# First layer of a two-layer cross-attention kernel: the exponential's scores made ahead of the maxima's scores in every step

## The chip, the cores and the metric

The kernel runs on one core of one Trainium2 chip. The metric is the device time of one execution in microseconds (us). Three runs of the kernel before gave 1755.6, 1747.01 and 1757.85 us, a median of 1755.6 us. The profiled execution that is read below took 1751.12 us, 1749.3 us of them inside the profile's span.

## The reference, cut to what matters

Eight batches of x (256 x 512) and of a context of the same shape go through two layers. Only the first one is touched. It attends along the last axis (512 positions) with 16 heads of 16 channels, and needs from the same weights both the mean and the standard deviation of the values:

```
q = Wq x + bq;  k = Wk ctx + bk;  v = Wv ctx + bv        # 16 heads, d = 16, 512 positions
attn = softmax(where(mask, (q / sqrt(d)) . k, -inf))      # 512 x 512 for each head
mean = attn . v;   ex2 = attn . (v * v)
std  = sqrt(relu(ex2 - mean * mean))
out  = (instance_norm(x) * std + mean) * mask
```

The second layer (self-attention, cross-attention and an MLP on 256 rows of 512 channels) follows and is left as it is.

## The kernel before, in words

**Groups and steps.** The first layer works on groups of four heads: 8 batches x 4 groups = 32 groups (`GROUPS`). A group has 8 steps: two pairs of heads, four blocks of 128 positions each. The program for TensorE is a written-out loop over windows `w` and steps `s` (the loop around lines 541 to 575), with `N = 8 * w + s`. Four sorts of TensorE work stand in it.

- `scores(N)` (line 510): two matmuls, one for each head of a pair, of 64 rows each on the upper and the lower half of the array, queries along the partitions. They fill two of four PSUM banks in turn. VectorE takes the maximum over the keys of each query from them (`maxima`, line 607). `scores(N)` waits until the maxima of step `N - 2` have freed its banks.
- `turned(M)` (line 519), with `M = N - 13`: the same products with the keys along the partitions, and with the negated maximum added through two extra rows of the query tile. Two matmuls of 64 rows, always into the same two banks. ScalarE turns them into the weights (`exponentials`, line 772). `turned(M)` waits until exponential `M - 1` has read the banks. Where `M` is a multiple of four it also waits for the maxima of the group to have come into the query tile by DMA (`s_top`).
- `weighted(M - 1)` (line 533): four matmul records of 128 rows that multiply the values and their squares by the weights of step `M - 1`. It waits for exponential `M - 1`, and at the start of a pair of heads until ScalarE has copied the pair before out of its bank (`v_out`, line 808).
- Items (`items_at`): in some steps one more product comes behind `weighted`. In windows with even `w` the projection of queries (`q`) stands in step 3 and that of keys (`k`) in step 6 (line 487); of values (`v`, line 496) there is one in step 6 of odd windows. In step 1 of each window from 1 on the maxima of the window before are turned by the identity (`turn`, line 501).

**ScalarE's order** (from line 771) is fixed too. In each step: for steps 4 and 7 of even windows first `high_of` (line 793), which takes the projection just made out of PSUM; then the exponential of that step; then what else belongs there, such as `take_values` (line 808), `take_turn` (line 801, which reads the turned maxima), the masks (line 780), or the square roots with two loads of a function table (line 832).

**The way of the maxima.** After group `w - 1` has its eight maxima, VectorE spreads them into `wide`, TensorE turns them in step 1 of window `w`, ScalarE copies the result to `top`, and SyncE's queue moves it by four small DMAs (`tops_in`, line 376) into the query tile. `turned` needs it in step 5 of the same window. On SyncE's queue these DMAs stand behind `rows_out` of the window before (line 342), and every fourth window that stands behind `shares_out`, which waits for a reciprocal on VectorE (line 664); this reciprocal comes behind the maxima of step 5 on that engine.

Before the first `turned` there are only `scores`, items and a few matmuls that fill time (line 540). Behind the last `scores` (`N = 255`) thirteen more steps of `turned` and `weighted` follow, together with the first items of the second layer.

Of the kernel before, what the change touches and what calls it, by code (L numbers as in the profile page):

```python
# [34 lines left out]
DMA = 16  # L35
# [49 lines left out]
def layer0(nc, d, g):  # L85

    GROUPS = NB * NG
# [13 lines left out]
    def items_at(w, s):  # L101

        if s in (3, 6) and w % 2 == 0 and w // 2 + 1 < PAIRS:
            return [("q" if s == 3 else "k", w // 2 + 1, (0, 1))]
        if s == turn_step(w) and 0 <= w - 1 < GROUPS:
            return [("turn", w - 1, (0, 1))]
        if s == 6 and w % 4 == 3 and w + 1 < GROUPS:
            return [("v", (w + 1) // 2, (0, 1))]
        if s == 6 and w % 4 == 1 and w < GROUPS:
            return [("v", w // 4 * 2 + 1, (0, 1))]  # L110
        if s == 4 and w == 0:
            return [("v", 0, (0, 1))]
        return []
# [5 lines left out]
    with ExitStack() as ctx:  # L119
# [3 lines left out]
        def sem(name):  # L123
            return g["whole"].enter_context(nc.semaphore("l0_" + name))
# [59 lines left out]
        s_top = [sem(f"top{p}") for p in range(2)]  # L184
# [6 lines left out]
        s_exp = sem("exp")  # L191
# [51 lines left out]
        def landed(eng, n):  # L243

            for name in "qk":
                eng.wait_ge(s_ring[name][n % RING], loads_of(n) * DMA)
# [22 lines left out]
        def rows_of(i):  # L269

            return slice(ROWS * i, ROWS * (i + 1))
# [183 lines left out]
    def tensor(eng, lead):  # L455
# [49 lines left out]
        def scores(N):  # L505

            n, j, p = N // 8, N % 4, N % 8 // 4
            for i in range(2):
                r = rows_of(i)
                mm = eng.matmul(ps[:, SC + 2 * (N % 2) + i, :], q_rows[r, n % RING, p, P * j:P * (j + 1)],  # L510
                                k_rows[r, n % RING, p, :], start=True, stop=True)
            mm.then_inc(s_score, 1)

        def turned(M):

            n, c, p = M // 8, M % 4, M % 8 // 4
            for i in range(2):
                r = rows_of(i)
                mm = eng.matmul(ps[:, ST + i, :], k_rows[r, n % RING, p, P * c:P * (c + 1)],  # L519
                                q_rows[r, n % RING, p, :], start=True, stop=True)  # L520
            mm.then_inc(s_st, 1)

        def weighted(M):

            n, c, p = M // 8, M % 4, M % 8 // 4
            b, G = n // NG, n % NG
            if c == 0:
                eng.wait_ge(s_sq, 2 * b + G // 2 + 1)
                if 2 * n + p:
                    eng.wait_ge(s_vout, 2 * n + p)  # L530
            eng.wait_ge(s_exp, M + 1)
            for k in range(2):
                mm = eng.matmul(ps[2 * QD * k:2 * QD * (k + 1), VB, :], v[:, c, HG * G + 2 * p + k, :],  # L533
                                prob[:, M % PROBS, k, :], start=(c == 0), stop=(c == DC - 1))
            mm.then_inc(s_pv, 1)

        def busy(count, bank, rows):

            for _ in range(count):
                eng.matmul(ps[:, bank, :], rows[:, 0:P], rows, start=True, stop=True)  # L540
# [6 lines left out]
        for w in range(GROUPS + 2):  # L547
            for s in range(8):
                N = 8 * w + s
                M = N - LAG  # L550
                if w < GROUPS:
                    if w == 0 and s in (0, 4):
                        eng.wait_ge(s_first_in[s // 4], 2 * DMA)
                    if w and s == 0:
                        landed(eng, w)
                    if N >= 2:
                        eng.wait_ge(s_max, N - 1)
                    scores(N)
                if N < 12:
                    busy((0, 0, 3, 2, 0, 8, 0, 7, 0, 0, 1, 1)[N], VB, k_rows[:, 0, 0, :])  # L560
                if 0 <= M < 8 * GROUPS:
                    if M % 4 == 0:
                        eng.wait_ge(s_top[M % 8 // 4], 2 * DMA * (M // 8 + 1))
                    if M:
                        eng.wait_ge(s_exp, M)
                    turned(M)
                if 0 <= M - 1 < 8 * GROUPS:
                    weighted(M - 1)
                lead(w, s, False)
                for x in items_at(w, s):  # L570
                    item(*x)
                lead(w, s, True)
# [311 lines left out]
    def gpsimd(eng):  # L884
# [56 lines left out]
        finish_x(LAST - 1, 1)  # L941

    return {"sync": sync, "tensor": tensor, "vector": vector, "scalar": scalar, "gpsimd": gpsimd}


# [1361 lines left out]
```

## Time and profile before

| | |
|---|---|
| median of three runs | 1755.6 us (1747.01 to 1757.85) |
| profiled execution | 1751.12 us, its span 1749.3 us |
| first layer's steps with `scores` and `turned` together | from 60 to about 608 us of the span |
| TensorE busy in the whole span | 1641.2 us, 94% |
| VectorE, ScalarE, GpSimd busy | 71%, 61%, 30% |

Times in the profile's rows are us from the span's start. A matmul's busy time is its own duration from issue to a modelled end, and neighbours overlap; what an operation costs the engine is the distance from its start to the next one's. A row of the time line merges the neighbours of one kind, so that "x2" is a pair of matmuls that run together. Weight loads are listed as an engine of their own (PEld).

### The profile page before, as it was taken

How to read it: one execution, taken by the hardware profiler on the slowest of the kernel's cores; microseconds unless marked ns; L12 is line 12 of the kernel's file. 1: busy time of each engine (PE TensorE's matmuls, PEld its weight loads, DVE VectorE, ACT ScalarE, POOL GpSimd, SP SyncE). 2: the span in 40 equal slices, each digit the busy share in tenths (PEclk: the TensorE clock that was granted, in tenths of full speed). 3: DMA queues.
4: the chain of work that ended last, by engine and by line, in shares of the span. 5: the costliest groups of instructions: out<-in, count | busy, mean ns of one | idle time of the engine just before them, and what ended most of it. 6: DMA issues, size and time to landing. Idle time of an engine off the chain costs nothing.

```text
span 1749.3 us, 30873 instructions
## 1 busy us (share of the span) xinstructions
PE 1641.2 (94%) x10589; PEld 1130.0 (65%) x10589; DVE 1242.7 (71%) x2758; ACT 1063.7 (61%) x2351; POOL 516.1 (30%) x795
## 2 busy tenths in 40 slices
PE   5999999999998988999999899999999899999999
PEld 3434334333343346788878678888888688888888
DVE  2676877778787838988999889999999762323222
ACT  1466766757666657778877878788887642111111
POOL 0135455654546523233223233333333220000000
PEclk7899999999999998999999999999999899999999
DMA  5555354553544413222233534333333330000000
GB/s 150 165 156 183 114 152 134 172 163 115 153 126 132 150 47 105 67 74 74 70 93 76 131 98 109 92 91 92 91 92 84 93 109 1 25 0 25 0 25 13
DMA packets 112556, 167.97 MB, mean 96 GB/s; under 512 B 27401, under 2 KB 43145, under 8 KB 112273
## 3 DMA queue, kind: packets, MB, share of 16 engines
q1 hardware_dynamic: 88720, 132.55, 26.1%
q0 software_dynamic: 20992, 29.12, 6.7%
q10 hardware_dynamic: 2688, 4.33, 0.9%
q8 instruction: 86, 1.41, 0.3%
q14 instruction: 70, 0.57, 0.1%
HBM read 72.06 MB, written 34.60 MB: 61 GB/s over the span
## 4 chain that ended last, share of the span: by engine, by line
PE 56%; DVE 21%; ACT 7%; issue 6%; DMA 5%; SPq 4%; POOL 0%; ACTq 0%; DVEq 0%; POOLq 0%
PE ps L533 11%; PE ps L1929 9%; PE ps L1903 7%; DVE at_t L1381 4%; DVE at_t L1386 4%; PE ps L510 4%; PE ps L1252 4%; PE ps L1262 4%; PE ps L519 3%; SPq L342 3%; PE ps L1201 2%; DMA ring<-top 2%; PE ps L1908 2%; PE ps L496 2%; ACT at_prob L1589 2%
## 5 line engine op out<-in xcount | busy, mean ns | idle before, releaser
L607 DVE TENSOR_REDUCE nmax<-ps 128x2 f32<-128x1024 f32 x256 | 310.0, 1221 | 144.1 <-PE ps L510 142.7
L772 ACT ACTIVATE prob<-ps 128x1024 f32<-128x1024 f32 x256 | 261.8, 1023 | 147.3 <-PE ps L519 142.8
L1589 ACT ACTIVATE at_prob<-at_t,at_nmax 128x256 f32<-128x256 f32 x512 | 256.6, 506 | 85.6 <-DVE at_nmax L1386 74.8
L533 PE MATMUL ps<-prob,v 128*64 128x512 f32 x1024 | 280.0, 625 | 2.0
L1386 DVE CUSTOM_DVE_ANT_0 at_t<-at_t,at_off 128x256 f32<-128x256 f32 x512 | 233.5, 492 | 8.8
L1747 POOL TENSOR_TENSOR at_low<-at_low,at_high 128x512 fp32r<-128x512 f32 x64 | 86.7, 1355 | 463.9 <-DVE at_high L1415 463.9
L2088 DVE CAST mlp_h_hi<-mlp_h 128x512 fp32r<-128x512 f32 x64 | 28.4, 444 | 213.0 <-ACT mlp_h L2000 179.9
L2000 ACT ACTIVATE mlp_h<-ps,b 128x512 f32<-128x512 f32 x48 | 33.1, 690 | 218.3 <-PE ps L1903 218.3
L510 PEld LDWEIGHTS ps<-ring 64*128 64x128 f32 x512 | 48.5, 187 | 168.1 <-issue 134.5
L1201 PE MATMUL ps<-ident,at_prob 128*128 128x128 f32 x1024 | 156.9, 276 | 0.0
L1381 DVE SCALAR_TENSOR_TENSOR at_t<-ps,mask_self 128x512 f32<-128x512 f32 x192 | 131.2, 684 | 19.5 <-PE ps L1190 19.0
L1190 PE MATMUL ps<-at_k_stack,at_q_stack 96*128 96x256 f32 x512 | 117.5, 312 | 29.1 <-ACT at_prob L1589 26.1
L510 PE MATMUL ps<-ring 64*128 64x512 f32 x512 | 130.2, 506 | 11.5 <-DMA ring<-rows 8.1
L519 PE MATMUL ps<-ring 64*128 64x512 f32 x512 | 109.4, 421 | 29.2 <-ACT prob L772 16.1
L300 POOL DMA_DIRECT2D sums<-v_out x120 | 60.3, 503 | 247.5 <-ACT v_out L808 247.5
L1201 PEld LDWEIGHTS ps<-ident,at_prob 128*128 128x128 f32 x1024 | 121.0, 142 | 0.2 <-issue 0.2
L1190 PEld LDWEIGHTS ps<-at_k_stack,at_q_stack 96*128 96x128 f32 x512 | 81.4, 191 | 59.6 <-ACT at_prob L1589 49.7
L1704 ACT ACTIVATE at_probT<-ps 128x512 f32<-128x512 f32 x192 | 112.1, 584 | 8.9 <-PE ps L1201 8.7
L533 PEld LDWEIGHTS ps<-prob,v 128*64 128x64 f32 x1024 | 51.8, 135 | 80.5 <-issue 80.5
L1589 ACT ACTIVATION_READ_ACCUMULATOR at_prob<-at_t,at_nmax 128x1 f32 x512 | 98.8, 193 | 0.0
L1252 PE MATMUL ps<-at_x_hi,w_lo 128*128 128x256 f32 x352 | 98.4, 280 | 0.0
L1214 PE MATMUL ps<-at_probT,at_v 128*32 128x128 f32 x2048 | 84.0, 282 | 0.6 <-ACT at_probT L1704 0.6
(218 smaller groups left out, 3915.5 us busy)
## 6 DMA issues: line engine op xcount, KB each, us to landing
ring<-rows SPq DMA_DIRECT2D x62, 512.0 KB, 5.5
rows<-shares_of SPq DMA_DIRECT2D x90, 256.0 KB
at_k_stack<-at_high SPq DMA_DIRECT2D x256, 64.0 KB, 2.5
at_q_stack<-at_high SPq DMA_DIRECT2D x128, 64.0 KB, 2.7
at_q_stack<-at_high POOLq DMA_DIRECT2D x128, 64.0 KB, 2.5
at_q_stack<-at_low SPq DMA_DIRECT2D x128, 64.0 KB, 2.3
at_k_stack<-at_low POOLq DMA_DIRECT2D x128, 64.0 KB, 2.3
c_in<-in_ctx SPq DMA_DIRECT2D x8, 512.0 KB, 8.5
```

What stands on the lines that cost most here:

```text
L510: mm = eng.matmul(ps[:, SC + 2 * (N % 2) + i, :], q_rows[r, n % RING, p, P * j:P * (j + 1)], k_rows[r, n % RING, p, :], start=True, stop=True)
L519: mm = eng.matmul(ps[:, ST + i, :], k_rows[r, n % RING, p, P * c:P * (c + 1)], q_rows[r, n % RING, p, :], start=True, stop=True)
L533: mm = eng.matmul(ps[2 * QD * k:2 * QD * (k + 1), VB, :], v[:, c, HG * G + 2 * p + k, :], prob[:, M % PROBS, k, :], start=(c == 0), stop=( ...
L607: eng.tensor_reduce(nmax[:, n % 2, j, 2 * p:2 * p + 2], ps[:, at:at + 2, :], AX, ALU.max, negate=True).then_inc(s_max, 1)
L772: eng.activation(prob[:, M % PROBS, :, :], ps[:, ST:ST + 2, :], ACT.Exp, scale=float(HD0) ** -0.5).then_inc(s_exp, 1)
L1190: mm = eng.matmul(ps[:, SC + p, S * i:S * (i + 1)], q[:, P * j:P * (j + 1)], k, start=True, stop=True)
L1201: mm = eng.transpose(ps[:, PT + m % 2, P * k:P * (k + 1)], prob[:, m % 2, i, P * c:P * (c + 1)], ident[:])
L1252: mm = eng.matmul(out, w[a][:, c, col], src[z_][:, c, :], start=(c == 0 and k == 0), stop=(c == DC - 1 and k == 2))
L1381: eng.scalar_tensor_tensor(out=t[:, i, :, :], in0=ps[:, SC + i, :].rearrange("p (h k) -> p h k", h=2), scalar=-SCALE, in1=masks[mask_of(ru ...
L1386: ins = eng.tensor_tensor_reduce(t[:, i, k, :], t[:, i, k, :], off[:, j, :], 1.0, NEVER, ALU.add, ALU.min, nmax[:, m % 4, k:k + 1])
L1589: ins = eng.activation(prob[:, m % 2, i, :], t[:, p, i, :], ACT.Exp, scale=-1.0, bias=nmax[:, m % 4, i:i + 1], accum_out=z[:, T % 2, j, 2 ...
L1929: mm = eng.matmul(ps[:, YB + SB * j + s, :], x[:, n % RING, i, P * s:P * (s + 1)], w2(w, share), start=(fresh and k == 0), stop=(final and ...
```

## The change

In each step of TensorE's written-out loop the block that issues `turned(M)`, with its waits, is moved from behind `scores(N)` to ahead of it. No instruction is added or removed in the other four queues, and their order is the same.

```diff
             for s in range(8):
                 N = 8 * w + s
                 M = N - LAG
+                if 0 <= M < 8 * GROUPS:
+                    if M % 4 == 0:
+                        eng.wait_ge(s_top[M % 8 // 4], 2 * DMA * (M // 8 + 1))
+                    if M:
+                        eng.wait_ge(s_exp, M)
+                    turned(M)
                 if w < GROUPS:
                     if w == 0 and s in (0, 4):
                         eng.wait_ge(s_first_in[s // 4], 2 * DMA)
@@
                     scores(N)
                 if N < 12:
                     busy((0, 0, 3, 2, 0, 8, 0, 7, 0, 0, 1, 1)[N], VB, k_rows[:, 0, 0, :])
-                if 0 <= M < 8 * GROUPS:
-                    if M % 4 == 0:
-                        eng.wait_ge(s_top[M % 8 // 4], 2 * DMA * (M // 8 + 1))
-                    if M:
-                        eng.wait_ge(s_exp, M)
-                    turned(M)
                 if 0 <= M - 1 < 8 * GROUPS:
                     weighted(M - 1)
                 lead(w, s, False)
```

TensorE's order around a turn of the maxima (L501) in step 1 of a window, before; L510 is `scores`, L519 `turned`, L533 `weighted`:

```order
L510 MATMUL ps<-ring 128x512 x2
L519 MATMUL ps<-ring 128x512 x2
L533 MATMUL ps<-prob,v 64x512 x2
L501 MATMUL ps<-ident_r,wide 128x128 x4
L510 MATMUL ps<-ring 128x512 x2
L519 MATMUL ps<-ring 128x512 x2
L533 MATMUL ps<-prob,v 64x512 x2
```

and in the changed kernel:

```order
L519 MATMUL ps<-ring 128x512 x2
L510 MATMUL ps<-ring 128x512 x2
L533 MATMUL ps<-prob,v 64x512 x2
L501 MATMUL ps<-ident_r,wide 128x128 x4
L519 MATMUL ps<-ring 128x512 x2
L510 MATMUL ps<-ring 128x512 x2
L533 MATMUL ps<-prob,v 64x512 x2
```

What follows an item or `weighted` directly is now `turned`, with its wait for ScalarE, and `scores` comes between `turned` and `weighted`.

The same engine at the end of a projection (L487, the last three of its six products) and in the step behind it, before:

```order
L487 MATMUL ps<-x_hi,w_hi 128x512
L487 MATMUL ps<-x_lo,w_hi 128x512
L487 MATMUL ps<-x_hi,w_lo 128x512
L510 MATMUL ps<-ring 128x512 x2
L519 MATMUL ps<-ring 128x512 x2
L533 MATMUL ps<-prob,v 64x512 x2
```

and in the changed kernel:

```order
L487 MATMUL ps<-x_hi,w_hi 128x512
L487 MATMUL ps<-x_lo,w_hi 128x512
L487 MATMUL ps<-x_hi,w_lo 128x512
L519 MATMUL ps<-ring 128x512 x2
L510 MATMUL ps<-ring 128x512 x2
L533 MATMUL ps<-prob,v 64x512 x2
```

Here too the pair behind the item is now the one that ScalarE reads; the pair that VectorE reads comes one place later.

## Rows read from the trace of the kernel before

**Rows 1.** The page: the span, and busy time of TensorE.

```profile
span 1749.3 us, 30873 instructions
PE 1641.2 (94%) x10589; PEld 1130.0 (65%) x10589; DVE 1242.7 (71%) x2758; ACT 1063.7 (61%) x2351; POOL 516.1 (30%) x795
```

**Rows 2.** Groups by line, 60 to 608 us: busy us, mean ns, idle before, releasers.

```profile
L607 DVE TENSOR_REDUCE nmax<-ps 128x2 f32<-128x1024 f32 x244 | 295.6, 1221 | 118.8 <-PE ps L510 117.5
...
L772 ACT ACTIVATE prob<-ps 128x1024 f32<-128x1024 f32 x242 | 247.4, 1023 | 128.4 <-PE ps L519 124.0
...
L501 PE MATMUL ps<-ident_r,wide 128*128 128x128 f32 x120 | 19.9, 288 | 0.0
L793 ACT ACTIVATE shares_of<-ps,b 128x512 fp32r<-128x512 f32 x28 | 19.2, 687 | 36.7 <-PE ps L487 36.7
L801 ACT ACTIVATE top<-ps 8x512 fp32r<-8x512 f32 x30 | 17.6, 586 | 0.0
L832 ACT ACT_TABLE_LOAD x6 | 7.7, 1283 | 0.1
```

**Rows 3.** Waits of TensorE's matmuls, 60 to 608 us: total, times, longest.

```profile
PE ps L519 <- ACT prob L772: 14.4, 12, 1.3
PE ps L519 <- DMA ring<-top: 13.0, 8, 3.5
```

**Rows 4.** Time line of plain steps: start, length, engine, line, operation.

```profile
305.90 1.23 DVE L607 TENSOR_REDUCE nmax<-ps 128x2 f32<-128x1024 f32 x1 [1.08 <-PE ps L510]
...
307.03 0.50 PE L510 MATMUL ps<-ring 64*128 64x512 f32 x2
...
307.37 0.40 PE L519 MATMUL ps<-ring 64*128 64x512 f32 x2
...
307.70 1.08 PE L533 MATMUL ps<-prob,v 128*64 128x512 f32 x4
307.81 1.02 ACT L772 ACTIVATE prob<-ps 128x1024 f32<-128x1024 f32 x1 [0.65 <-PE ps L519]
...
308.71 0.50 PE L510 MATMUL ps<-ring 64*128 64x512 f32 x2
...
308.88 0.19 PEld L519 LDWEIGHTS ps<-ring 64*128 64x128 f32 x2
```

**Rows 5.** Time line behind a projection of keys.

```profile
299.70 0.50 PE L510 MATMUL ps<-ring 64*128 64x512 f32 x2
...
299.81 0.69 ACT L793 ACTIVATE shares_of<-ps,b 128x512 fp32r<-128x512 f32 x1 [1.72 <-PE ps L487]
...
300.48 1.02 ACT L772 ACTIVATE prob<-ps 128x1024 f32<-128x1024 f32 x1
...
301.56 0.19 PEld L519 LDWEIGHTS ps<-ring 64*128 64x128 f32 x2
```

**Rows 6.** Time line behind a turn of the maxima.

```profile
304.77 0.66 PE L501 MATMUL ps<-ident_r,wide 128*128 128x128 f32 x4
...
305.37 0.50 PE L510 MATMUL ps<-ring 64*128 64x512 f32 x2
305.47 0.59 ACT L801 ACTIVATE top<-ps 8x512 fp32r<-8x512 f32 x1
...
306.14 1.02 ACT L772 ACTIVATE prob<-ps 128x1024 f32<-128x1024 f32 x1
```

**Rows 7.** Time line where `turned` came late: TensorE and ScalarE.

```profile
312.37 0.50 PE L519 MATMUL ps<-ring 64*128 64x512 f32 x2 [1.49 <-DMA ring<-top]
312.79 1.08 PE L533 MATMUL ps<-prob,v 128*64 128x512 f32 x4
...
312.90 1.02 ACT L772 ACTIVATE prob<-ps 128x1024 f32<-128x1024 f32 x1 [1.45 <-PE ps L519]
```

**Rows 8.** Stretches with such a wait: busy us of each engine, granted clock, DMA share.

```profile
308.00:318.00 10.00, 8.43 (x48) 3.88 (x44) 6.09 (x8) 5.44 (x6) 9.98 (x16) 1.00 0.79 265
...
528.00:538.00 10.00, 6.41 (x23) 1.78 (x20) 5.05 (x6) 4.48 (x5) 8.88 (x14) 0.83 0.76 244
```

## The prediction, as it was put on record

> **What bounds the kernel now.** I read the page first, for the share of each engine [rows 1]: TensorE is busy 94% of the span. A busy share does not tell what a single edit is worth, so I went to the stretch in which the moved work runs, 60 to 608 us, and looked at who is idle and for whom [rows 2]. VectorE's maxima were preceded by 118.8 us of idle time, nearly all of it waiting for `scores`; ScalarE's exponentials by 128.4 us, nearly all of it waiting for `turned`. Both engines wait for TensorE. The other way round TensorE waited little [rows 3]: 12 times for an exponential (14.4 us) and 8 times for the turned maxima to land (13.0 us). So the stretch is bound by the sum of TensorE's work, with some 27 us of waits on top, all of them at `turned`.
>
> Then the time line of a plain step [rows 4]. `scores` starts at 307.03, `turned` at 307.37 (0.34 later), `weighted` at 307.70 (0.33), the next `scores` at 308.71 (1.01). A step is 1.68 us. In it the exponential starts at 307.81, which is 0.78 behind the start of `scores`, and ends at 308.83; the weights of the next `turned` are loaded at 308.88, 0.05 later. That is already 0.17 behind the start of the next `scores`. It costs nothing, since `scores` is running on the array then. **This is the point to see: today `scores` covers the last 0.17 us of ScalarE's work in each step.**
>
> **The change, part by part.** Nothing is added or removed. The cyclic order of the three parts goes from scores, turned, weighted to turned, scores, weighted. I call the moment at which the first of the three can start the head of the step.
>
> *The plain step: nothing.* TensorE's sum stays 0.34 + 0.33 + 1.01 = 1.68 us; both pairs have the same shape. `turned` now starts at the head. Where a `turned` starts with nothing of `scores` ahead of it today, the exponential follows 0.53 behind it (312.37 to 312.90) [rows 7]. The ScalarE loop is then 0.53 + 1.02 + 0.05 = 1.60 us [rows 4, 7], 0.08 less than TensorE's 1.68. TensorE goes on as the bound, and the exponential starts 0.78 - 0.53 = 0.25 earlier in the step. What is lost is the cover: ScalarE's deadline moves forward too, from 0.17 behind the head to the head. Where the exponential's start is set by `turned` both shifts cancel. Where it is set by something else on ScalarE, only the deadline moves, and TensorE stands still.
>
> *Behind a projection.* `high_of` is issued ahead of the exponential and ends at 299.81 + 0.69 = 300.50; the exponential starts at 300.48, so both the copy and `turned` hold it there today [rows 5]. With `turned` first it could start at 299.70 + 0.53 = 300.23, but the copy still ends at 300.50. It ends at 301.52, the next weights load at 301.57, the same moment as today (301.56 in the row). Today `scores` starts at 299.70 + 1.68 = 301.38 ahead of it; then nothing does. TensorE loses 0.19 us. There are 28 such copies in the stretch [rows 2]. Twelve of them cost nothing of their own: six stand ahead of a window in which `turned` waits for the maxima's DMA anyway, six lie in the shadow of the square roots (six loads of the table for them [rows 2]). 16 x 0.19 = 3.0 us.
>
> *Behind a turn of the maxima.* `take_turn` starts at 305.47 and ends at 306.06; the exponential starts at 306.14, set by `turned` [rows 6]. With `turned` at 305.37 it would be ready at 305.90, but ScalarE is held to 306.06. It ends at 307.08, the weights load at 307.13, against a head at 307.03 [rows 4, 6]: 0.10 lost. Of 30 turns (30 copies of `top` [rows 2]) 8 are in windows with a DMA wait and 6 in those with roots: 16 x 0.10 = 1.6 us.
>
> *Where `turned` waits long already.* Today `scores` is done before the wait, and `weighted` starts 0.42 behind `turned` (312.37, 312.79) [rows 7]. After the change `scores` is behind the same wait, and turned plus scores take 0.34 + 0.33 = 0.67 [rows 4]. The release of the wait hangs on ScalarE or on a DMA and does not move. So each wait costs 0.25 more: 12 + 8 times [rows 3], 20 x 0.25 = 5.0 us.
>
> *The maxima.* `scores` leaves 0.25 later in the step, so VectorE starts its maxima later. The next user of the banks is two steps away: the reduction that started at 305.90 ended at 307.13, and its banks are written again at 308.71, 1.58 later [rows 4]. That covers it. But every fourth window the reciprocal behind the maxima of step 5 starts the row of DMAs that ends with the late landing. I take 0.25 for seven windows, 1.8 us.
>
> SyncE's and GpSimd's queues keep their order; their DMAs follow the events above. The second layer, the start and the thirteen last steps, which have no `scores`, stay as they are. No term is a gain.
>
> **The sum:** 3.0 + 1.6 + 5.0 + 1.8 = 11.4 us. The profiled execution took 1751.1 us, so by its own time 1762.5. The median of the three runs is 4.5 us above that execution; I put the sum on the median: 1755.6 + 11.4 = **1767 us**.
>
> Two prices the trace doesn't show. *A restart after a short stop:* a late `turned` took 0.42 to the next work, a covered one 0.33 [rows 4, 7]. If these 0.09 are also paid when `scores` follows, the 52 places above cost 52 x 0.09 = 4.7 us more. I take 0, since `scores`, itself first behind `weighted`, hands over in 0.34. *The clock:* below.
>
> The Trainium skill ("TensorE: Matmul & The Clock Gate", the section on the mechanism of row and column tiling) says that a weight load overlaps running matmuls only where it goes to other rows of the array. `weighted` uses all rows, so by this rule the load of whichever pair comes first behind it stands open, and that of the second pair runs under the first. The trace agrees as far as it goes: `turned` loads at 308.88 while `scores` of 308.71 runs.
>
> **The rivals.**
>
> *Nothing happens (chance 0.20).* The plain step is a balance, and if ScalarE's copies can start a little earlier than I read, or the waits absorb one another, the terms shrink to 0 to 4 us: 1756 to 1760. For it: the same sum of work, the same other queues. Against: 0.19 and 0.10 are read directly from ScalarE's rows.
>
> *Faster: ScalarE's loop was the bound (0.07).* In the plain step the weights of `turned` load 0.05 behind the end of the exponential [rows 4], as if TensorE were waiting there. Putting `turned` first shortens that loop from 1.68 to 1.60. If TensorE's work could follow, some 190 plain steps (242 exponentials [rows 2] less the 52 places) would gain 0.08 each: 15 us, 1740. It decides if TensorE's hand-over times of 0.34 and 0.33 hide waiting. Against it: the step behind the turn, in which the exponential was long done, has the same length (305.37 to 307.03, 1.66) [rows 4, 6].
>
> *Worse: the load stands open in every step (0.13).* If `turned` at the head pays the 0.09 in plain steps too, because its weights can't be prepared before ScalarE's signal, 242 x 0.09 = 22 us come on top: 1789. The rule of the skill above would give this if the gap were open only for a pair that waits. The trace shows `scores`, which has to wait for nothing, only.
>
> *Worse: the clock (0.10).* After the longest wait the clock fell: 528 to 538 us has a mean granted clock of 0.83, where 308 to 318 has 1.00 with a shorter wait [rows 8]. With two levels, 1.2 and 2.4 GHz, 0.83 is half speed for about 3.4 us, a loss of 1.7 us. The change leaves TensorE idle 0.25 to 0.5 longer in the seven windows of this kind. Four more falls cost 7 us: 1774.
>
> **Chances and range.** The forecast (1760 to 1775) has 0.50. The range goes from 1751 (nothing happens, and the base nearer to the profiled execution) to 1781 (the forecast with the restarts and the clock); it leaves out the faster case and the full open load. A measurement of this kernel can tell about 1% (17.5 us) from no change. Slower by more than that: most of the open load, half of the clock, the top of the forecast: 0.23. Faster by more: 0.03. Within: 0.74.
>
> **What the changed profile would show.** In plain steps `turned` first, `scores` 0.34 later, `weighted` 0.33 after that, and the same 1.68; exponentials 0.53 behind the head. Behind a projection the weights of the next `turned` load some 0.19 behind the head with TensorE idle; behind a turn 0.10. Waits of `turned` for the exponential rise from 12 to over 40 in number. `weighted` starts 0.67 behind a late `turned`. The maxima's idle time stays about what it is. I am wrong if the plain step is not 1.68, or if those short stops are absent.

## The result and the profile after

| | before | changed |
|---|---|---|
| median of 7 runs | 1750.73 us (1745.71 to 1757.85) | 1764.51 us (1761.33 to 1770.79) |
| profiled execution, its span | 1751.12 us, 1749.3 us | 1762.39 us, 1760.6 us |
| mean granted clock of the profiled execution | 0.979 | 0.977 |

The changed kernel takes 1.0079 of the time before, with a 95% interval of 1.0059 to 1.0099. That is 13.8 us by the medians and 11.3 us between the two profiled spans. The forecast was 1767 us and 11.4 us more. The change is smaller than the 1% that the prediction held for the least that can be told, yet its interval is clear of no change.

The page of the changed kernel, for [rows 1]:

```profile
span 1760.6 us, 30873 instructions
...
PE 1643.7 (93%) x10589; PEld 1119.6 (64%) x10589; DVE 1249.2 (71%) x2758; ACT 1056.2 (60%) x2351; POOL 516.4 (29%) x795
```

The same instructions and nearly the same busy time in a span that is 11.3 us longer: time was added as idle time of TensorE and as slower matmuls, not as work. Seen by the 256 records of `weighted`, nearly all of it lies in the steps:

```profile
64.25 1.97 PE L533 MATMUL ps<-prob,v 128*64 128x512 f32 x4
```

```profile
62.30 1.98 PE L533 MATMUL ps<-prob,v 128*64 128x512 f32 x4
```

These are the first ones, before and changed. The last one starts at 658.85 before and at 668.88 in the changed kernel. So the steps between them take 12.0 us more, what lies ahead of them 2.0 us less, and what follows them 1.3 us more. The groups by line, 60 to 620 us, for [rows 2]:

```profile
L607 DVE TENSOR_REDUCE nmax<-ps 128x2 f32<-128x1024 f32 x243 | 294.8, 1221 | 128.1 <-PE ps L510 126.9
...
L772 ACT ACTIVATE prob<-ps 128x1024 f32<-128x1024 f32 x244 | 248.3, 1018 | 121.9 <-PE ps L519 121.3
L519 PE MATMUL ps<-ring 64*128 64x512 f32 x488 | 124.4, 504 | 40.4 <-ACT prob L772 19.8 <-DMA ring<-top 18.8
L510 PE MATMUL ps<-ring 64*128 64x512 f32 x486 | 99.7, 401 | 0.0
```

The two products have changed places in their mean length too: the first pair behind `weighted` is the long one (504 ns; its record starts together with that of its weight load), the second the short one (401 ns). ScalarE waits a little less for TensorE and VectorE a little more. The waits of TensorE in the same stretch, first the matmuls' [rows 3], then those of the weight loads, columns as there:

```profile
PE ps L519 <- ACT prob L772: 19.8, 12, 2.1
PE ps L519 <- DMA ring<-top: 18.8, 10, 2.7
```

```profile
PEld ps L519 <- ACT prob L772: 111.9, 111, 3.0
```

The weight load of `turned` now stands at a wait for ScalarE 111 times (19 times before, 20.4 us), but only twelve of these are waits of the matmuls too. In the others the array still has the product before to work on. Those twelve grew from 14.4 to 19.8 us, the waits for the maxima from 13.0 to 18.8 us.

A plain step, for [rows 4]:

```profile
308.84 0.50 PE L519 MATMUL ps<-ring 64*128 64x512 f32 x2
...
309.18 0.40 PE L510 MATMUL ps<-ring 64*128 64x512 f32 x2
...
309.38 1.02 ACT L772 ACTIVATE prob<-ps 128x1024 f32<-128x1024 f32 x1 [0.62 <-PE ps L519]
...
309.50 1.08 PE L533 MATMUL ps<-prob,v 128*64 128x512 f32 x4
...
310.51 0.50 PE L519 MATMUL ps<-ring 64*128 64x512 f32 x2
```

`turned`, 0.34 later `scores`, 0.32 later `weighted`, and the next `turned` 1.67 behind the first: the plain step is as long as before. The exponential starts 0.54 behind the head, that is, behind the start of `turned`.

Behind the projection of keys, for [rows 5]:

```profile
301.43 0.50 PE L519 MATMUL ps<-ring 64*128 64x512 f32 x2
```

```profile
301.54 0.69 ACT L793 ACTIVATE shares_of<-ps,b 128x512 fp32r<-128x512 f32 x1 [1.89 <-PE ps L487]
302.12 1.01 ACT L772 ACTIVATE prob<-ps 128x1024 f32<-128x1024 f32 x1
```

```profile
303.19 0.19 PEld L519 LDWEIGHTS ps<-ring 64*128 64x128 f32 x2 [0.90 <-ACT prob L772]
```

The step is 1.76 us here (301.43 to 303.19), where a plain one is 1.67: 0.09 lost, not 0.19. The exponential starts at 302.12, though the copy ahead of it ends at 301.54 + 0.69 = 302.23: neighbours on ScalarE overlap by 0.1 us. Behind the turn, for [rows 6]:

```profile
307.27 0.59 ACT L801 ACTIVATE top<-ps 8x512 fp32r<-8x512 f32 x1
...
307.76 0.99 ACT L772 ACTIVATE prob<-ps 128x1024 f32<-128x1024 f32 x1
```

The exponential starts 0.10 ahead of the copy's end and is through at 308.75; the next `turned` starts at 308.84, 1.68 behind the one of 307.16. Nothing is lost here.

A late landing, for [rows 7]:

```profile
314.65 0.79 PE L519 MATMUL ps<-ring 64*128 64x512 f32 x2 [2.40 <-DMA ring<-top]
315.24 0.63 PE L510 MATMUL ps<-ring 64*128 64x512 f32 x2
315.80 1.97 PE L533 MATMUL ps<-prob,v 128*64 128x512 f32 x4
```

TensorE stood idle for 2.40 us (1.49 before), and `weighted` takes 1.97 us instead of 1.08: the clock has fallen. The stretches around the late landings of windows 11 to 27 (four of the five, the one left out has 0.81), for [rows 8]; the clock is the third number from the end:

```profile
236.00:242.00 6.00, 3.59 (x14) 1.00 (x12) 4.22 (x5) 2.73 (x5) 5.54 (x9) 0.79 0.75 244
312.00:318.00 6.00, 3.60 (x12) 1.09 (x12) 4.14 (x5) 2.22 (x4) 5.33 (x8) 0.72 0.69 239
...
462.00:468.00 6.00, 3.40 (x12) 1.09 (x12) 5.82 (x5) 2.13 (x3) 4.01 (x6) 0.73 0.80 255
537.00:543.00 6.00, 3.57 (x12) 0.98 (x12) 4.21 (x5) 2.29 (x4) 5.40 (x9) 0.74 0.81 268
```

and in the kernel before, four of the six from window 7 to 27 (the other two have 1.00):

```profile
165.00:171.00 6.00, 4.50 (x16) 1.18 (x14) 3.46 (x5) 3.47 (x4) 5.98 (x11) 0.74 0.85 264
...
310.00:316.00 6.00, 4.42 (x23) 1.54 (x20) 4.12 (x5) 4.09 (x5) 5.98 (x10) 1.00 0.80 256
383.00:389.00 6.00, 4.49 (x15) 1.31 (x16) 3.58 (x5) 3.16 (x4) 5.99 (x10) 0.77 0.85 242
...
531.00:537.00 6.00, 4.07 (x12) 1.18 (x14) 1.57 (x2) 1.93 (x3) 4.88 (x8) 0.72 0.84 248
```

The clock fell behind three of six late landings before, and behind five of six in the changed kernel (in window 7 it did not). It fell once more there behind the landing of window 31, at 611.5 us, where it had stayed up before. A stretch of 6 us at 0.72 is half speed for 3.4 us and costs about 1.7 us. From 60 to 620 us half speed cost 9.6 us before and 12.9 us in the changed kernel, counted in stretches of half a microsecond.

The length of a stop alone does not decide a fall. Before, the clock fell behind stops of TensorE of 1.50, 1.56 and 3.51 us and stayed up behind 1.44, 1.49 and 2.20 us. In the changed kernel it fell behind five stops of 2.08 to 2.60 us at landings, and stayed up behind all five stops of 2.06 to 2.08 us that are shown next.

Last, the stop that grew most by itself, the wait behind the masks (five of them). Before:

```profile
208.61 0.50 PE L510 MATMUL ps<-ring 64*128 64x512 f32 x2
...
209.57 0.63 ACT L780 ACTIVATE mask<-m_in 128x512 f32<-128x512 uint8 x1 [2.93 <-DVE X L681]
...
212.07 0.50 PE L519 MATMUL ps<-ring 64*128 64x512 f32 x2 [1.30 <-ACT prob L772]
...
212.51 1.08 PE L533 MATMUL ps<-prob,v 128*64 128x512 f32 x4
```

and in the changed kernel:

```profile
205.80 0.50 PE L519 MATMUL ps<-ring 64*128 64x512 f32 x2
...
207.11 0.63 ACT L780 ACTIVATE mask<-m_in 128x512 f32<-128x512 uint8 x1 [3.46 <-DVE X L681]
...
209.61 0.50 PE L519 MATMUL ps<-ring 64*128 64x512 f32 x2 [2.08 <-ACT prob L772]
...
210.28 1.08 PE L533 MATMUL ps<-prob,v 128*64 128x512 f32 x4
```

From the head of the step to `weighted` of the next it took 3.90 us, now 4.48. ScalarE's mask starts 0.96 behind the head before and 1.31 after, since it waits for VectorE, whose work ahead of it (L681, which stands in its queue with the maxima) ends 0.35 later. The rest is `scores` behind the late `turned`: 0.67 to `weighted` instead of 0.44.

### The profile page after: what moved, and what is told of

Read it like the earlier page. It is cut to its first block, busy times and chain, and to the rows that moved or that the text cites. A ratio compares the mean times of both kernels' runs of the same rounds, so it can differ in the third digit from the quotient of the medians.

```text
span 1760.6 us, 30873 instructions
## 1 busy us (share of the span) xinstructions
PE 1643.7 (93%) x10589; PEld 1119.6 (64%) x10589; DVE 1249.2 (71%) x2758; ACT 1056.2 (60%) x2351; POOL 516.4 (29%) x795
## 4 chain that ended last, share of the span: by engine, by line
PE 54%; DVE 21%; ACT 7%; issue 7%; DMA 5%; SPq 4%; POOL 0%; ACTq 0%; DVEq 0%; POOLq 0%
PE ps L533 9%; PE ps L1929 9%; PE ps L1903 7%; PE ps L519 5%; PE ps L1252 4%; DVE at_t L1381 4%; DVE at_t L1386 4%; PE ps L1262 4%; DMA ring<-top 3%; PE ps L1201 2%; SPq L342 2%; PE ps L510 2%; PE ps L1908 2%; PE ps L1190 2%; ACT at_prob L1589 2%
## 5 line engine op out<-in xcount | busy, mean ns | idle before, releaser
L533 PE MATMUL ps<-prob,v 128*64 128x512 f32 x1024 | 283.7, 632 | 1.6
L519 PEld LDWEIGHTS ps<-ring 64*128 64x128 f32 x512 | 50.1, 187 | 207.0 <-ACT prob L772 113.8
L519 PE MATMUL ps<-ring 64*128 64x512 f32 x512 | 130.7, 505 | 42.1 <-ACT prob L772 21.5
L510 PE MATMUL ps<-ring 64*128 64x512 f32 x512 | 106.8, 410 | 9.8 <-DMA ring<-rows 8.0
L533 PEld LDWEIGHTS ps<-prob,v 128*64 128x64 f32 x1024 | 52.2, 137 | 97.0 <-issue 97.0
```

## The experiments

Ratios are against the kernel before, run on the same chip in the same series, with a 95% interval. The expectations name four theories. A: the loss sits at the long waits. B: it is spread over all steps (for the edit of the queue below, B stands for something else: that only the waits go and the falls of the clock stay). C and D, from the second series on, differ in what a long stop costs beyond its length. C says that the clock is the larger part of the loss, since longer stops make it fall more often; D says that the loss is the waits' own length and the falls are chance.

**The order in one step, or in all but one.** The block of `turned` is issued ahead of `scores` where a condition on the step holds, and behind it elsewhere:

```diff
+                if 0 <= M < 8 * GROUPS and s == 5:
+                    ...
+                    turned(M)
                 if w < GROUPS:
...
-                if 0 <= M < 8 * GROUPS:
+                if 0 <= M < 8 * GROUPS and not (s == 5):
                     ...
                     turned(M)
```

Step 5 alone:

> `turned` goes ahead of `scores` only in step 5 of each window, where it waits for the turned maxima to land; in the other seven steps the order is that of before. Theory A (the loss sits at the long waits): eight late landings at 0.4 to 0.6 us more each, 4 us, and about three more falls of the clock at 1.7 us, 5 us: 1750.7 + 6 to 11 = 1757 to 1762. Theory B (the loss is spread over all steps, since a `turned` at the head has its weight load open): an eighth of 13.8 us, 1752 to 1753.

Measured: 1766.64 us against 1752.08, 1.0082 (1.0054 to 1.0110).

All but step 5 (`s != 5`):

> `turned` first in all steps but step 5. Theory A: the waits for the exponential behind the masks cost 5 x 0.5 to 0.6 us, the stops behind projections 1 to 3 us, no more clock falls than before: 1750.7 + 3 to 6 = 1754 to 1757. Theory B: seven eighths of the loss, 1762 to 1763.

Measured: 1770.54 us against 1752.08, 1.0106 (1.0085 to 1.0128).

All but steps 0 and 5 (`s not in (0, 5)`):

> `turned` first in steps 1, 2, 3, 4, 6 and 7 alone; in step 5 (landing of the maxima) and step 0 (behind the masks and behind the projection of keys) the order is that of before. Theory A: what is left are short stops behind turns and square roots, 0 to 2 us: 1751 to 1753, no difference that can be told. Theory B: six eighths of the loss, 1761.

Measured: 1767.55 us against 1752.08, 1.0092 (1.0070 to 1.0115).

None of the three fits A or B: each part costs as much as the whole or more. The time line of the first shows what the expectations had left out:

```profile
221.45 0.40 PE L519 MATMUL ps<-ring 64*128 64x512 f32 x2
221.78 1.08 PE L533 MATMUL ps<-prob,v 128*64 128x512 f32 x4
223.06 0.50 PE L519 MATMUL ps<-ring 64*128 64x512 f32 x2 [0.20 <-ACT prob L778]
```

Where the order switches from scores-first to turned-first, two `turned` follow each other without `scores` between them. TensorE has 0.33 + 1.01 = 1.34 us of work for a ScalarE loop of 1.6, and `weighted` to `turned` takes 1.28 instead of 1.01. The step with the switch takes 1.94 us where it took 1.71: 0.23 us in each of 29 windows, some 7 us. In the third kernel (`s not in (0, 5)`) the same comes in step 1, 1.94 instead of 1.71. Behind step 5 of the second and the third kernel a switch costs nothing in total: step 6 takes 1.85 instead of 1.82, step 5 1.67 instead of 1.71. So in all but step 5 the switch is no explanation. What its trace shows more of is half speed: it cost 17.0, 18.8 and 15.3 us from 60 to 620 us in the three kernels, in their order here, against 9.6 in the kernel before and 12.9 in the changed one. The cost of the order is not a sum over steps, so this trio can't place it.

**A transfer taken out of the row that ends with the landing.** In the changed kernel `rows_out("q")` goes ahead of `shares_out`:

```diff
+            if w % 2 == 0 and ahead < PAIRS:
+                rows_out("q", ahead)
             if w % NG == 2 and b >= 0:
                 shares_out(b)
             if w % 2 == 0 and ahead < PAIRS:
-                rows_out("q", ahead)
                 rows_out("k", ahead)
```

> The changed kernel with one edit on SyncE's queue: the three DMAs that write the rows of the queries out go ahead of `shares_out`, which waits for the reciprocal, so that they no longer stand in the row that ends with the late landing of the maxima. Theory A: that landing comes some 3.5 us earlier, the waits of `turned` for it (18.8 us in the changed kernel) shrink to under 3 us and the clock falls with them: 1764.5 - 16 to 24 = 1740 to 1748. Theory B: only the waits go, and the clock falls stay: 1764.5 - 13 to 16 = 1748 to 1752. A rival to both: the queue is held by something else and the landing does not move, 1764.

Measured: 1771.27 us against 1752.08, 1.0112 (1.0089 to 1.0134). A miss for A and B, and nearest to the rival, though slower than it. The queue of SyncE:

```profile
301.11 2.02 SPq L342 DMA_DIRECT2D rows<-shares_of  x3
303.18 1.33 SPq L414 DMA_DIRECT2D shares<-z  x1
309.66 1.28 SPq L419 DMA_DIRECT2D rz<-shares  x2
311.11 1.85 SPq L342 DMA_DIRECT2D rows<-shares_of  x3
313.00 4.96 SPq L376 DMA_DIRECT2D ring<-top  x4
```

The small `shares<-z` (32 KB) now follows three writes of 256 KB, and the loads that wait for its landing are issued 6.5 us behind it; in the changed kernel that was 1.7 us (298.83 and 300.49). The row became longer.

**The loads of `rz` taken out of it.** They and their waits (`shares_back`, split off from `shares_out`) go one window later, behind `tops_in`:

```diff
             if 0 <= w - 1 < GROUPS:
                 tops_in(w - 1)
+            if w % NG == 3 and b >= 0:
+                shares_back(b)
```

> The changed kernel with the loads of `rz` (two DMAs that wait for a round trip through memory) moved on SyncE's queue from ahead of the six DMAs of `rows_out` to behind the DMAs of the maxima one window later. Theory C: the maxima land 2.5 to 3 us earlier, the long waits in step 5 (18.8 us) shrink to under 6 us and the falls behind them go: 1764.5 - 15 to 22 = 1743 to 1750. Theory D: the waits alone, 1764.5 - 12 = 1752.

In the changed kernel. Measured: 1809.58 us against 1755.16, 1.0313 (1.0298 to 1.0328).

> The same move of the two loads in the kernel before. The waits for the maxima (13.0 us) go to under 3 us. Theory C: their three falls of the clock go too: 1751 - 12 to 16 = 1735 to 1739. Theory D: 1751 - 10 = 1741. If `turned` first costs only where the waits are, the two kernels with this move lie 3 to 7 us apart instead of 13.8.

In the kernel before. Measured: 1794.96 us against 1755.16, 1.0227 (1.0212 to 1.0242). Both are misses for C and D. The waits for the maxima did shrink, to 3.0 and 1.0 us, but a new wait took their place, in the same window (kernel before with the move):

```profile
323.40 1.02 ACT L778 ACTIVATE prob<-ps 128x1024 f32<-128x1024 f32 x1 [0.65 <-PE ps L525]
331.68 1.06 ACT L833 ACTIVATE std_a<-mean_a 128x1024 f32<-128x1024 f32 x1 [7.25 <-POOL mean_a L900]
```

ScalarE squares the mean that GpSimd makes from `rz`, and the exponentials stand behind this in its queue. I had counted GpSimd's slack and missed who waits for it. The new waits make the pair a poor test of the order. It does say that the two orders stay apart with the waits for the maxima nearly gone: 1.0313 / 1.0227 = 1.0084, 15 us.

**Work in place of the stop.** Six matmuls that nobody needs are worked ahead of the wait in step 5 of six windows:

```diff
+                if w % NG == 3 and 3 < w < GROUPS - 2 and s == 5:
+                    eng.wait_ge(s_max, N - 1)
+                    busy(6, SC + 2 * (N % 2), w_hi0[:, 0, :])
```

> The changed kernel with six more matmuls of 512 columns (fixed weights, into the bank of the next `scores`, 1.3 to 1.5 us of work in all) ahead of the wait for the maxima in step 5 of six windows (7, 11, ..., 27), where TensorE stands idle for 1.5 to 3 us. Their results are overwritten. Theory C (the clock is the larger part of the loss: the longer stops make it fall more often): TensorE works through most of the wait, the falls behind these waits go, 4 to 8 us gained: 1757 to 1761. Theory D (the loss is the waits' own length, as in the sum of the prediction, and the falls are chance): no gain, 1764 to 1767.

In the changed kernel. Measured: 1766.64 us against 1755.16, 1.0065 (1.0050 to 1.0080).

> The same six matmuls ahead of `scores` in step 5 of the same windows of the kernel before. Theory C: the three falls behind these waits in its trace go as well, 3 to 5 us gained, less for the later `scores`: 1746 to 1749. Theory D: no gain, 1751 to 1754.

In the kernel before. Measured: 1747.83 us against 1755.16, 0.9965 (0.9952 to 0.9979). Here it is a gain that is clear of zero, 6 us by the interval's middle, though it only adds work: the lowest ratio of all versions. The gain is the clock: the mean granted clock of its six executions is 0.982, against 0.976 in the eleven of the kernel before beside them. So stops do cost by the clock, as C says of them. In the changed kernel the same edit gained next to nothing (1.0065, where the order alone is 1.0079). Its stretches, one at a late landing and one behind the masks:

```profile
313.00:319.00 6.00, 5.92 (x38) 3.08 (x36) 2.68 (x3) 3.00 (x4) 4.89 (x8) 1.00 1.02 337
358.00:364.00 6.00, 6.00 (x24) 1.81 (x20) 3.23 (x5) 3.56 (x5) 0.99 (x3) 0.72 0.00 0
```

Behind the landings of windows 7 to 23 the clock now stays up; behind those of 27 and of 31, where no matmuls were added, it still fell. It fell behind the masks instead, four times, where it had not fallen in the changed kernel's trace. These stops are as long as there, 2.08 us, so it is not their length that changed. The changed order has two kinds of stops of 2 us and more in each four windows, and taking one away left the other. Against C speaks that this kernel's mean clock (0.978 over six executions) is no lower than that of the kernel before beside it (0.976), and it still takes 11.5 us more: here the clock is not the larger part of the loss.

**The masks moved.** ScalarE makes the next mask one window later, behind the exponential of a step in which TensorE has a projection:

```diff
-                if s == 6 and w % NG == 1 and b + 1 < NB:
+                if s == 3 and w % NG == 2 and b + 1 < NB:
                     masks(b + 1)
```

> The kernel before, with ScalarE's making of the next mask moved from step 6 of a window (where it waits for VectorE, and five exponentials behind it with it) to step 3 of the next one. Five waits of `turned` of 1.3 us each go: 1752 - 6 to 8 = 1744 to 1746 by either theory, 1 to 3 less if some falls of the clock hung on them (theory C).

In the kernel before. Measured: 1755.77 us against 1753.37, 1.0014 (0.9994 to 1.0034).

> The same move in the changed kernel. Theory D (the loss is the added length of the waits): it gains what the kernel before gains plus 5 x 0.58 = 3 us; it stays some 11 us behind that kernel with the move. Theory C: the same, since the falls behind the landing of the maxima remain; 1764.5 - 10 = 1754.

In the changed kernel. Measured: 1759.19 us against 1753.37, 1.0030 (1.0012 to 1.0048).

The kernel before gained nothing, against both theories, though its waits for the exponential went from 14.4 to 9.6 us. The next stops took it back. Four of the five waits (1.56 us each) are gone by window 23, and still this `turned` starts only 0.5 us earlier than in the kernel before (458.69):

```profile
453.56 0.50 PE L510 MATMUL ps<-ring 64*128 64x512 f32 x2
458.21 0.79 PE L519 MATMUL ps<-ring 64*128 64x512 f32 x2 [4.15 <-DMA ring<-top]
458.93 1.97 PE L533 MATMUL ps<-prob,v 128*64 128x512 f32 x4
```

The waits for the maxima rose to 16.0 us, with falls of the clock behind them. The mean clock of its twelve executions is 0.974, against 0.978 in the 35 of the kernel before beside them.

The distance between the two orders is 1.0030 / 1.0014 = 1.0016, by the two intervals about 0.27% either way, against 1.0079 without the move. It refutes D's 11 us, and B. It is a miss for C too, which had put the changed kernel at 1754 and the other at 1745 or below. And it does not show that the order has become harmless, for the clock moved the other way here: the kernel with the old order lost more of it (0.974) than the one with the new order (0.976), though the latter's waits for the maxima are longer (22.8 us in its trace, against 16.0). In that trace the clock stayed up behind a stop of 3.33 us.

**Both edits.**

> The kernel before with both edits: masks moved, and six matmuls worked in step 5 of six windows while it waits for the maxima. Theory C: no long stop of TensorE is left, next to no fall of the clock in the first layer: 1738 to 1743.

In the kernel before. Measured: 1747.10 us against 1753.37, 0.9977 (0.9961 to 0.9993), short of the 1738 to 1743 of C.

> The changed kernel with both edits. Theory C: with the long stops gone or filled the order of the two products is nearly indifferent; what is left is 0.14 us behind seven and 0.09 us behind fourteen projections, 2.3 us, and some 0.3 us at each landing of the maxima, 2 us: 3 to 6 us behind the kernel before with both edits. Theory D, or a cost in the plain steps: still 10 to 14 us behind it.

In the changed kernel. Measured: 1756.40 us against 1753.37, 1.0016 (0.9999 to 1.0033). The distance between the orders is 1.0016 / 0.9977 = 1.0039, some 0.23% either way: 6.9 us, between the 3 to 6 us of C and the 10 to 14 of D, and its interval (2.8 to 10.9 us) touches both. In the profile of the first TensorE has its full clock nearly everywhere (0.99 from 60 to 620 us); in the second, waits for the maxima of 17.7 us are left, one of them 5.9 us long.

**The clock of every execution.** Each execution beside the experiments, and each of the changed kernel, has a mean granted clock on record, and not only the profiled ones. Within one kernel an execution with a clock lower by 0.001 took 1.07 us more (a line through all 157 executions, each measured from its own kernel's mean, give or take 0.2). With this the distances between the orders can be compared at equal clock. Old order means `scores` first, new order `turned` first. In the first row 0.9776 is the mean of the 57 executions of the kernel before beside the experiments. The last column is an estimate, good to some 4 us:

| edit made to both | distance, us | mean clock, old and new order | distance at equal clock, us |
|---|---|---|---|
| none | 13.8 | 0.9776, 0.9750 | 11 |
| six matmuls in the stop | 17.6 | 0.9822, 0.9777 | 13 |
| loads of `rz` later | 15 | 0.9676, 0.9612 | 8 |
| masks moved | 2.8 | 0.9737, 0.9758 | 5 |
| masks moved, six matmuls | 6.9 | 0.9799, 0.9792 | 6 |

Some 3 of the 13.8 us are the clock, and most of the rest is there at any clock. In both pairs without the wait behind the masks the orders are nearer to each other, but 5 to 6 us stay.

## Why the prediction was right, point by point

- *The plain step costs nothing.* Right: 1.67 us, same hand-over times, the exponential 0.54 behind the head. With it fall both rivals on the plain step, the gain of 15 us and the open weight load of 22 us.
- *Behind projections, 3.0 us.* The step is real, but the price is too large and the places are too few. The loss is 0.09 behind the keys, in 14 windows, and 0.14 behind the queries, in 8, read from the distance of successive `weighted`: 2.4 us. The 0.1 us by which an operation on ScalarE starts ahead of the end of the one before was not in my sum, though [rows 5] had it: the copy ends at 300.50 and the exponential starts at 300.48.
- *Behind turns, 1.6 us.* Wrong, 0. The same overlap covers all of the 0.10. By the prediction's own last sentence the absence of the short stops counts against it, and here they are absent.
- *The long waits, 20 x 0.25 = 5.0 us.* The price is right where the release is fixed: `weighted` 0.67 behind a late `turned`, before 0.42 to 0.44. But the release was not fixed everywhere. Behind the square roots (six places) ScalarE's own row had moved forward by 0.2, so they cost 0.04 each. Behind the masks (five) it moved back by 0.35, through VectorE, and they cost 0.58 each, 2.9 us. This is the step of the prediction that failed in kind: I let VectorE's delay count only for the reciprocal.
- *The reciprocal, 0.25 for seven windows.* Half at its source: it starts 1.92 behind the head of step 5 where it had been 1.80. At the landings nothing of it can be told: from the `weighted` before to the late `turned` it takes 3.0 to 5.2 us before and 3.0 to 3.7 us in the changed kernel in windows 7 to 27, 21.0 and 20.4 us in sum.
- *The clock, held outside the sum at a chance of 0.10.* This was under-weighted. In the two traces the mean clock of 0.977 against 0.979 is 0.002 x 1760 = 3.5 us, a third of the distance between them; over all executions (0.9750 and 0.9776) it is an estimated 3 us. It made up for terms that were too large.
- *Waits for the exponential, from 12 to over 40.* Wrong for the matmuls (still 12), right for the weight loads only (19 to 111). The maxima's idle time, said to stay, grew from 118.8 to 128.1 us.
- *The weight loads.* The prediction says that the trace agrees with the rule of the Trainium skill ("TensorE: Matmul & The Clock Gate", the mechanism of row and column tiling). It does not, in the words that the prediction gives the rule. `scores` and `turned` both use both halves of the rows, and the load of `turned` at 308.88 stands beside `scores` of 308.71 on the same rows [rows 4], as far as records with modelled ends can tell. No term of the sum hangs on it.
- *The top of the range.* 1767 + 4.7 + 7 is 1779, not 1781. Nothing hangs on that either.

So the sum came out near the measurement (11.4 against 11.3 between the profiles and 13.8 by the medians), with some 7 us of direct stops, about 3.5 us of clock and 1.1 us at one turn of the maxima that VectorE had ready late. That the sum is so near is in part luck: a term of 1.6 us that is nothing and others that were too large stood against a clock that it left out, and against 2 us that the changed kernel gained ahead of its first `weighted`, which no term had. The 1767 us has luck of its own: its base, the median of three runs, was 4.9 us above the median of seven, and the sum 2.4 us below the measured distance.

Shown: the plain step is neutral; the short stops behind projections and the longer ones behind masks and landings are there, each with its price in the trace; filling a stop with useless work makes the kernel before faster, with the clock up. Only argued: the clock's share in the median, an estimate from the executions' mean clocks; that the wait behind the masks is half of the cost of the order, since moving it also changed the landings and the clock; and why the clock falls behind one stop and not behind another of the same length, which stays open.

## What to carry to other kernels

When a consumer's product is moved to the head of a step, look for what else holds that consumer: in steps in which it waits for nothing but the product the move is free, in the others the moved product had been standing behind a cover. Price a stop of TensorE by what the clock does behind it as well as by its length, and look at the mean clock of every execution before a difference is put down to an edit. And a stop ahead of a transfer that is late anyway is not worth removing until that transfer is earlier.

## What the runs showed of the hardware

- Adding six matmuls of 512 columns in each of six stops (1.66 us for one set) lowered the time by 0.35%, and the mean granted clock was 0.982 instead of 0.976.
- The clock fell behind stops of TensorE of 1.50 us and stayed up behind one of 3.33 us. Each fall cost 1.7 us, or 3.4 us where half speed lasted twice as long.
- Operations in ScalarE's queue overlap by 0.1 us when they follow without a wait: a copy from 307.27 to 307.86, the exponential from 307.76.
- A small write behind three of 256 KB took 6.5 us until the loads that wait for it were issued, against 1.7 us where these writes came behind it.
